# An attention block with an 8-bit product, written out without loops and with its fills cut into 16 parts a step

## The chip, the core and the metric

The kernel runs on one core of one Trainium2 chip. The time is device microseconds from start to end of one execution. Times given "at x" are microseconds from the start of the span of one profiled execution. Engines are named as in the profile: PE is TensorE (PEld its weight loads), DVE is VectorE, ACT is ScalarE, POOL is GpSimd, SP is SyncE, whose queue starts most DMAs.

## What is computed

For each of 8 batches `x` is 512 tokens by 256 features, and `cond` holds two style vectors `s1` and `s2`. Cut to what matters:

```python
x = x * s1[:, None, :]
x = (x - mu) * rsqrt(var + EPS_IN)                  # per token
q = heads(einsum('bsh,oh->bso', x, q_weight) * q_dc[:, None, :])
k = heads(einsum('bsh,oh->bso', x, k_weight) * k_dc[:, None, :])
v_flat = einsum('bsh,oh->bso', x, v_weight) * v_dc[:, None, :] * s2[:, None, :]
attn = softmax(einsum('bhqd,bhkd->bhqk', q, k) * scale)       # 16 heads of 16
out = einsum('bhqk,bhkd->bhqd', attn, heads(v_flat))...
out = einsum('bsh,oh->bso', out, w_weight) * w_dc[:, None, :]
y = out + einsum('bsh,oh->bso', v_flat, u_weight) * u_dc[:, None, :]
# y is rounded to int8 per token, rhs to int8 per column; their product is scaled back
return x_in + int8_product(y, rhs)
```

## The kernel before

The work is in 8 steps, one batch each, after a prologue. All five engines run programs of their own and meet at counting semaphores. Each engine works strictly in the order of its own program.

**A step** `t` has 16 rounds, 4 for each group of 4 heads. A round `r` has on PE `scores_of` (L939: four products into four PSUM banks, in two units of two), which I write S, and `values_of` (L953: four products that add to `o_acc`), which I write V. ACT takes the exponential of each unit of S (L493) into `probs`. The scores of a unit may be overwritten when its exponential is done, so S of round r+1 needs the exponentials of round r unit by unit. PE runs S of round r and then V of round r-1. `probs` has 2 buffers.

**Saving a group.** After the four rounds of a group ACT copies `o_acc` to `o_t` (`save_o`, L479), once V of the group's last round is done. It stands in ACT's program behind both exponentials of rounds 4, 8, 12 and of round 0 of the next step. V of the next group waits for it.

**Fills.** Behind V of certain rounds PE runs other work, the fills, through three banks of `work`. `claimed` lets PE be three uses ahead of DVE, which frees the banks in order. For the next batch, `a = t+1`: `xt` (the transposes of normalised x), `q` and `k` projections (L976, six products for one of two groups), `fold` (L985), `v` (L997, four token blocks of six products), `norms` (L1006) with a transpose of its maximum. For the batch before, `z = t-1`: `on` (16 transposes of `o_t` by token block, and DVE divides by the softmax sum), `ot` (back to features), `y` (L1087, the output projection), `yqt` (the transposed integers) and `ffn` (L1101, the integer product). All transposes are L815.

**Stacks.** ACT (L473) and DVE (L684, L688) split each q and k into a high and a low part in `parts`. SP copies these by 24 DMAs a batch (L322) into `q_stack` and `k_stack`, the operands of S. A flag, computed by DVE from the norms, says whether the scores are small enough to need no shift. If they are (they are here), SP copies zeros into two rows of `q_stack` (L311), between the third and fourth of its four lots of stack DMAs (the second and third in the prologue). The other branch, which computes row maxima, is jumped over.

**Loops.** Steps 1 to 6 are a loop of 3 turns with 2 steps in its body, on every engine; the prologue, step 0 and step 7 stand outside it. At the start of a step SP loads x of the next batch (L254), and DVE multiplies and measures it (L539, L545) before anything else of that step.

**The end.** Behind the last V, ACT saves the last group and the whole chain `on`, `ot`, `y`, `yqt`, `ffn`, residual (POOL, L439) and store of batch 7 runs with nothing beside it.

Of the kernel before, what the change touches and what calls it, by code (L numbers as in the profile page):

```python
# [5 lines left out]
F32 = mybir.dt.float32  # L20
# [7 lines left out]
P = 128  # L28
# [11 lines left out]
class Tally:  # L40

    def __init__(self, sem):
        self.sem, self.base, self.count = sem, 0, 0

    def value(self):
        return self.base + self.count

    def loop(self, index, per_turn):
        self.start, self.per_turn = self.value(), per_turn  # L50
        self.base, self.count = index * per_turn + self.start, 0

    def end_loop(self, turns):
        assert self.count == self.per_turn, (self.count, self.per_turn)
        self.base, self.count = self.start + turns * self.per_turn, 0

def adaln_ffn_kernel(nc, x, cond, wq, wk, wv, ww, wu, rhs, out):
# [15 lines left out]
    SETUP_USES, ROW_USES, RHS_USES, A_USES, Z_USES = 7, 2, 3, 12, 12  # L74
    STEP_USES = A_USES + Z_USES
# [3 lines left out]
    SHIFT = 2 * 2 * 16  # L79

# [4 lines left out]
    with ctx:  # L85
# [3 lines left out]
        def sem(name):  # L89
            return ctx.enter_context(nc.semaphore(name))  # L90

# [28 lines left out]
        col_now = sb("col_now", [P, 4])  # L120
# [11 lines left out]
        v_aug = sb("v_aug", [P, 2, KT, NH, DV])  # L132
# [6 lines left out]
        probs = sb("probs", [P, 2, 4, S])  # L139
        o_t = sb("o_t", [P, G, S])  # L140

# [8 lines left out]
        inv_den = sb("inv_den", [P, KT, NH])  # L150
        o_nat = sb("o_nat", [P, KT, H])
        o_t2 = sb("o_t2", [P, HC, S])
# [3 lines left out]
        y_scale = sb("y_scale", [P, KT])  # L156
        y_inv = sb("y_inv", [P, KT])
        y_q = o_nat
# [5 lines left out]

        by_two = [o_t2[:, :, :].rearrange("p c t -> p (c t)").rearrange("p (m c i) -> p m c i", m=2, c=HC),
# [16 lines left out]
        shift_loaded = sem("shift_loaded")  # L182
        pool_setup, const_ready = sem("pool_setup"), sem("const_ready")
# [5 lines left out]
        col_ready, wvs_ready, wd_ready = sem("col_ready"), sem("wvs_ready"), sem("wd_ready")  # L189
# [14 lines left out]

        FULL = ([("on", q) for q in range(KT)] + [("ot", i) for i in range(2)] + [("xt", c) for c in range(HC)]
                + [("rows", n) for n in range(ROW_USES)] + [("rhs", n) for n in range(RHS_USES)]
                + [("y", 0), ("y", 1), ("q", 0), ("k", 0), ("q", 1), ("fold", 0), ("k", 1), ("v", 0), ("bound", 0)]
                + [("v", k) for k in range(1, KT)] + [("yqt", i) for i in range(2)] + [("ffn", 0), ("ffn", 1)])
        A_KINDS = ("xt", "fold", "q", "k", "bound", "v")
        assert len(FULL) == STEP_USES + ROW_USES + RHS_USES  # L210

        def uses(has_a, has_z, prologue=False):
            def kept(kind):

                own = {"rows": prologue, "rhs": not prologue and not has_z}
                return own[kind] if kind in own else has_a if kind in A_KINDS else has_z

            return {u: n for n, u in enumerate([u for u in FULL if kept(u[0])])}

        def uses_before(t):  # L220

            return t * STEP_USES + (FIRST_STEP + A_USES + RHS_USES - STEP_USES)

        FIRST_STEP = SETUP_USES + A_USES + ROW_USES

        PAIRS = (B - 2) // 2

        def run_steps(eng, step, tally=None, per_turn=0):
            step(None, 0, has_a=True, has_z=False, base=SETUP_USES, bank=SETUP_USES, prologue=True)  # L230
            step(0, 0, has_a=True, has_z=False, base=FIRST_STEP, bank=FIRST_STEP)
            with eng.Fori(0, PAIRS) as pair:
                if tally is not None:
                    tally.loop(pair, per_turn)
                for odd in range(2):
                    t = pair * 2 + (1 + odd)
                    step(t, (1 + odd) % 2, has_a=True, has_z=True, base=uses_before(t), bank=uses_before(1 + odd))
            if tally is not None:
                tally.end_loop(PAIRS)
            step(B - 1, (B - 1) % 2, has_a=False, has_z=True, base=uses_before(B - 1), bank=uses_before(B - 1))  # L240

        LAST_Z = uses_before(B - 1) + Z_USES
        LAST_AT = {use: LAST_Z + n for n, use in enumerate(
            [("on", q) for q in range(KT)] + [("ot", 0), ("ot", 1), ("y", 0), ("y", 1), ("yqt", 0), ("ffn", 0),
                                              ("yqt", 1), ("ffn", 1)])}

        block = ctx.enter_context(nc.Block())

        @block.sync
        def _(sp):
# [7 lines left out]

            sp.sem_inc(res_added, 2)
# [5 lines left out]
            sp.wait_ge(demod_rows_ready, 1)  # L267
            sp.dma_start(rows_dram[:, :, :], demod_rows[:, :, :]).then_inc(rows_stored, 16)
            sp.wait_ge(rows_stored, 16)
            load_rows(0)  # L270
            sp.wait_ge(pool_stored, 16)
            sp.wait_ge(const_stored, 16)
            for par in range(2):
                for e in range(2):
                    sp.dma_start(k_stack[e * HALF + BIAS:e * HALF + ROWS, par, :, :].bitcast(F32), const_dram[1]
                                 ).then_inc(ones_loaded, 16)
            sp.wait_ge(xt_ready, 2)
            load_x(1)
# [6 lines left out]
            def step(t, par, has_a, has_z, base, bank, prologue=False):  # L285
                a = 0 if prologue else t + 1
                pa = 0 if prologue else 1 - par
                if has_a:
                    if not prologue:
                        wait(v_ready, a * KT)  # L290
                        wait(wd_ready, a)
                        if has_z:
                            wait(xt_ready, a * 2)
                            load_x(a)
                        load_rows(a)
                if has_z:
                    z = t - 1
                    wait(res_added, z * 2 + 2)
                    sp.dma_start(x_res[:, :, :], x[z].rearrange("(k p) h -> p k h", p=P)).then_inc(res_loaded, 16)
                if has_a:  # L300
                    if not prologue and not (isinstance(t, int) and t == 0):
                        wait(exp_done, t * UNITS)

                    for n in range(4):
                        if n == (2 if prologue else 3):

                            wait(flag_ready, a + 1)
                            small = sp.value_load(flag[0:1, 0:1], min_val=0, max_val=1)
                            with sp.If(small == 1):
                                for e in range(2):  # L310
                                    sp.dma_start(q_stack[e * HALF + BIAS:e * HALF + ROWS, pa, :, :].bitcast(F32),  # L311
                                                 const_dram[0]).then_inc(shift_loaded, SHIFT // 2)
                            sp.nop()
                        g, is_k = n // 2, n % 2
                        stack, which = (k_stack, K_PARTS) if is_k else (q_stack, Q_PARTS)
                        for part, part_ready in enumerate((hi_ready, low_ready)):
                            wait(part_ready, a * 4 + (n + 1))
                            for j in range(NB):
                                if which[j] == part:
                                    for e in range(2):  # L320
                                        rows_of = slice(e * HALF + j * D, e * HALF + (j + 1) * D)
                                        sp.dma_start(stack[rows_of, pa, g * GP:(g + 1) * GP, :].bitcast(F32),  # L322
                                                     parts[e * HALF:(e + 1) * HALF, n, part, :].bitcast(F32)
                                                     ).then_inc(stack_loaded[g], 16)
                    with sp.If(small == 0):
                        wait(shift_ready, a + 1)
                        for j in range(2):
                            for e in range(2):
                                row = e * HALF + BIAS + j
                                sp.dma_start(q_stack[row:row + 1, pa, :, :].bitcast(F32),  # L330
                                             shift[e * NP:(e + 1) * NP, j, :].bitcast(F32)
# [825 lines left out]
```

## Time and profile before

| what | value |
|---|---|
| median of 3 runs | 498.12 us (497.38 to 498.86) |
| the profiled execution's own time | 496.59 us |
| its span, first to last instruction | 494.9 us |
| mean granted TensorE clock | 0.962 |
| PE busy | 447.1 us (90%) |
| ACT busy | 290.1 us (59%) |
| DVE busy | 241.7 us (49%) |
| POOL busy | 103.6 us (21%) |

A group of instructions in a row has its start, its time from the first start to the last end, and in brackets how long its engine sat idle before it and what ended that wait.
### The profile page before, as it was taken

To read this page: it belongs to the slowest core of one execution; us is meant where nothing else is said; L and a number is where in the kernel's file an instruction comes from. 1 tells how busy PE (TensorE), PEld (TensorE's weight loads), DVE (VectorE), ACT (ScalarE), POOL (GpSimd) and SP (SyncE) were. 2 spreads that over 40 slices of the span, in tenths; PEclk is the share of its full clock that TensorE was granted. 3 is DMA by queue.
4 is the path that set the end of the run, shared out by engine and by line. 5 is a ranking of instruction groups with operands and counts; after the bars stand their busy time and mean duration, and the time that the engine had idled before them with its cause. 6 is when DMAs were issued, how large, how long until landed. Compare 5 with 4: busy or idle time off the path is not lost.

```text
span 494.9 us, 8739 instructions
## 1 busy us (share of the span) xinstructions
PE 447.1 (90%) x2626; PEld 225.3 (46%) x2626; DVE 241.7 (49%) x564; ACT 290.1 (59%) x333; POOL 103.6 (21%) x124
## 2 busy tenths in 40 slices
PE   6892899979999999969999999969999999999982
PEld 5771235434554455524454455424554455544251
DVE  4766142346444763446434763447444763444054
ACT  4030587556765766637765766647765766677930
POOL 5442003010121303031121303031121303020022
PEclk9997699998999999979999999989999999999997
DMA  6068309660497209650397209660497209620021
GB/s 208 0 149 176 68 1 137 109 146 1 62 129 159 88 20 134 107 177 0 57 130 145 105 12 139 107 182 0 64 128 158 87 22 135 106 88 1 1 86 42
DMA packets 29804, 45.31 MB, mean 92 GB/s; under 512 B 3928, under 2 KB 15448, under 8 KB 29704
## 3 DMA queue, kind: packets, MB, share of 16 engines
q1 hardware_dynamic: 27840, 40.02, 45.6%
q0 software_dynamic: 1072, 3.74, 1.9%
q8 instruction: 32, 0.52, 0.5%
q10 hardware_dynamic: 832, 0.80, 0.5%
q14 instruction: 28, 0.23, 0.2%
HBM read 15.09 MB, written 4.28 MB: 39 GB/s over the span
## 4 chain that ended last, share of the span: by engine, by line
PE 78%; issue 5%; ACT 5%; DMA 5%; DVE 5%; SPq 2%; POOL 1%; POOLq 0%; ACTq 0%; DVEq 0%
PE o_acc L953 22%; PE scores L939 16%; PE work L976 10%; PE work L997 9%; PE work L815 8%; PE work L1087 6%; ACT probs L493 4%; PE work L985 3%; DMA q_stack<-const_dram 2%; PE work L844 2%; PE work L1101 1%; DMA x_res<-in_L_cond_w_weight_dram 1%; DVE o_nat L749 1%; DMA rows<-in_cond_dram 1%; SPq L322 1%
## 5 line engine op out<-in xcount | busy, mean ns | idle before, releaser
L493 ACT ACTIVATE probs<-scores 128x1024 f32<-128x1024 f32 x256 | 247.9, 1026 | 129.0 <-PE scores L939 128.8
L953 PE MATMUL o_acc<-probs,v_aug 128*32 128x512 f32 x1024 | 140.7, 622 | 0.2
L939 PE MATMUL scores<-q_stack,k_stack 50*128 50x512 f32 x512 | 103.2, 467 | 26.7 <-DMA q_stack<-const_dram 10.9
L939 PEld LDWEIGHTS scores<-q_stack,k_stack 50*128 50x128 f32 x512 | 41.0, 191 | 81.9 <-issue 37.2
L420 POOL TENSOR_TENSOR squares<-parts 128x512 bf16<-128x512 f32 x32 | 33.3, 1041 | 185.5 <-ACT parts L473 185.5
L976 PE MATMUL work<-x_t,qk_w 128*128 128x512 f32 x192 | 54.3, 421 | 0.0
L997 PE MATMUL work<-vs_w,x_t 128*128 128x512 f32 x192 | 50.9, 407 | 0.3 <-DVEq L680 0.3
L439 POOL TENSOR_TENSOR res<-res,x_res 128x512 f32<-128x512 f32 x16 | 20.0, 1270 | 136.6 <-DVEq L799 136.6
L976 PEld LDWEIGHTS work<-x_t,qk_w 128*128 128x128 f32 x192 | 35.2, 193 | 24.1 <-issue 6.7
L997 PEld LDWEIGHTS work<-vs_w,x_t 128*128 128x128 f32 x192 | 34.2, 188 | 23.4 <-issue 13.9
L953 PEld LDWEIGHTS o_acc<-probs,v_aug 128*32 128x32 f32 x1024 | 20.5, 109 | 49.1 <-issue 45.5
L1087 PE MATMUL work<-w_demod,o_t 128*128 128x256 f32 x128 | 31.5, 390 | 0.0
L1087 PEld LDWEIGHTS work<-w_demod,o_t 128*128 128x128 f32 x128 | 23.1, 189 | 14.3 <-DVEq L767 5.0
L643 DVE TENSOR_TENSOR v_aug<-work,rows 128x256 f32<-128x256 f32 x32 | 13.5, 423 | 28.3 <-PE work L997 28.1
L688 DVE SCALAR_TENSOR_TENSOR parts<-work,col_now,parts 128x512 fp32r<-128x512 f32 x16 | 12.0, 751 | 30.7 <-ACT parts L473 27.2
L815 PE MATMUL work<-ident,o_t 128*128 128x128 f32 x136 | 21.1, 297 | 4.6 <-DVEq L752 2.8
L815 PEld LDWEIGHTS work<-ident,o_t 128*128 128x128 f32 x136 | 15.6, 149 | 19.6 <-issue 10.9
L815 PE MATMUL work<-ident,o_nat 128*128 128x128 f32 x128 | 19.6, 292 | 4.5 <-DVE o_nat L777 2.4
L473 ACT ACTIVATE parts<-work,col_now 128x512 fp32r<-128x512 f32 x16 | 11.0, 688 | 21.5 <-PE work L976 21.5
L782 DVE TENSOR_SCALAR y_qt<-work 128x512 bf16<-128x512 f32 x14 | 9.7, 691 | 28.3 <-PE work L815 26.1
L815 PEld LDWEIGHTS work<-ident,o_nat 128*128 128x128 f32 x128 | 14.3, 145 | 18.9 <-DVEq L752 7.1
L539 DVE TENSOR_TENSOR x_sb<-x_sb,rows 128x1024 f32<-128x1024 f32 x8 | 10.5, 1312 | 24.0 <-DMA rows<-in_cond_dram 12.6
(110 smaller groups left out, 389.4 us busy)
## 6 DMA issues: line engine op xcount, KB each, us to landing
q_stack<-parts SPq DMA_DIRECT2D x96, 128.0 KB, 5.3
k_stack<-parts SPq DMA_DIRECT2D x96, 128.0 KB, 5.5
x_sb<-in_x_dram SPq DMA_DIRECT2D x8, 512.0 KB, 5.4
x_res<-in_x_dram SPq DMA_DIRECT2D x8, 512.0 KB, 3.9
out_dram<-res POOLq DMA_DIRECT2D x7, 512.0 KB, 4.7
rows<-rows_dram SPq DMA_DIRECT2D x8, 384.0 KB, 5.5
rows<-in_cond_dram SPq DMA_DIRECT2D x8, 128.0 KB, 5.3
q_stack<-const_dram SPq DMA_DIRECT2D x16, 32.0 KB
```

Source lines behind the costliest of these rows:

```text
L420: nc.gpsimd.tensor_tensor(squares[:, n, :], parts[:, n, 0, :], parts[:, n, 0, :], ALU.mult).then_inc(squares_ready, 1)
L439: nc.gpsimd.tensor_tensor(res[:, two, :], res[:, two, :], x_res[:, two, :], ALU.add).then_inc(res_added, 1)
L493: nc.scalar.activation(probs[:, r % 2, pair:pair + 2, :], scores[:, pair:pair + 2, :], ACT.Exp).then_inc(exp_done, 1)
L643: nc.vector.tensor_tensor(v_aug[:, pa, k, :, 0:D], both[:, 0:H].rearrange("p (h d) -> p h d", d=D), rows[:, 1, :].rearrange("p (h d) -> p ...
L688: nc.vector.scalar_tensor_tensor(parts[:, n, 1, :], bank_qk, col_now[:, g:g + 1], parts[:, n, 0, :], ALU.mult, ALU.subtract).then_inc(low_ ...
L815: return nc.tensor.transpose(dst, src, ident[0:rows, 0:rows])
L939: last = nc.tensor.matmul(scores[:, 2 * (u % 2) + e, :], k_stack[top:top + ROWS, par, 2 * g + u % 2, kt * P:(kt + 1) * P], q_stack[top:top ...
L953: last = nc.tensor.matmul(o_acc[DV * j:DV * (j + 1), :], v_aug[:, par, kt, 4 * g + j, :], probs[:, r % 2, j, :], start=(kt == 0), stop=(kt ...
L976: last = nc.tensor.matmul(bank, lhs, right, start=(n == 0), stop=(n == len(operands) - 1))
L985: last = nc.tensor.matmul(bank[:, hc * H:(hc + 1) * H], wv_scaled[:, c, hc * P:(hc + 1) * P], w_t[WU][:, c, :], start=(c == 0), stop=(c == ...
L997: last = nc.tensor.matmul(bank, lhs, right, start=(n == 0), stop=(n == len(operands) - 1))
L1087: last = nc.tensor.matmul(bank[:, k * H:(k + 1) * H], lhs, right, start=(n == 0), stop=(n == len(operands) - 1))
```

## The change

- All loops are gone: each engine's program is written out for 8 steps. Waits are on constants.
- The 16 rounds are handled as 8 pairs `i`. In a pair PE runs S of round 2i, V, the first part of a fill, then `second_round()` (S of round 2i+1 and V), then the second part. So all 16 gaps between rounds can hold a part, listed in `fill`.
- V is one round later: behind S of round r comes V of round r-2. `probs` has 3 buffers.
- `save_o` in pairs 2, 4, 6 and in pair 0 stands between the exponentials of the two rounds of the pair.
- Of a batch's values only block 0 is projected in the step before; blocks 1 to 3 come in pairs 0 and 1 of its own step, just before V needs them. `v_aug` has one buffer instead of two.
- `on` goes by head group: four transposes as soon as a group is saved, so groups 0 to 2 are handled in their own step (pairs 3, 5, 7) and group 3 in pair 0 of the next. DVE's `normalise` takes a group for all tokens.
- `ffn` of a batch moves a step later (pairs 4 and 5 of step z+2).
- x of batch t+2 is loaded in step t, multiplied, measured and normalised there, so that `xt` in pair 1 finds it ready.
- SP writes the zeros at the start of a step whatever the flag says, and at the end of its stack DMAs only adds to the semaphore if the flag is set.

The core of the diff (of both programs only the lines that the text speaks of):

```diff
-        probs = sb("probs", [P, 2, 4, S])
+        probs = sb("probs", [P, RING, 4, S])
...
-        run_steps(pe, step)
...
-                for r in range(ROUNDS):
-                    scores_of(t, par, r, has_z)
-                    if r > 0:
-                        values_of(t, par, r - 1, has_z)
...
+            for t in range(B):
+                for i in range(SUPER):
+                    r = t * ROUNDS + 2 * i
+                    scores_of(r)
+                    if r > 0:
+                        values_of(r - 2)
+
+                    def second_round():
+                        scores_of(r + 1)
+                        if r > 0:
+                            values_of(r - 1)
+
+                    fill(t, i, second_round)
...
+                elif i == 2:
...
+                        if not first:
+                            to_features(z, 0)
+                        projected("q", a, 0)
+                        second_round()
+                        projected("k", a, 0)
...
+                elif i == 4:
...
+                        if y >= 0:
+                            int_product(y, 0)
+                        projected("k", a, 1)
+                        second_round()
+                        if not first:
+                            output(z, 0)
...
+                elif i == 6:
...
+                        if not first:
+                            quantised_transposed(z, 0)
+                            output(z, 1)
+                        second_round()
+                        norms(a)
...
-                    if r % KT == 0 and r > 0:
-                        save_o(t, r // KT - 1)
-                    if r == 0 and has_z:
-                        save_o(t - 1, G - 1)
...
+                for i in range(SUPER):
+                    exponentials(t * ROUNDS + 2 * i)
+                    if i == 0 and t > 0:
+                        save_o(t * G - 1)
+                    if i in (2, 4, 6):
+                        save_o(t * G + i // 2 - 1)
+                    exponentials(t * ROUNDS + 2 * i + 1)
```

Three places show how the instructions move. **ACT, rounds 0 to 9 of step 0** (`probs` is written by the exponentials, two for a round; `o_t` by `save_o`; `parts` are the high parts), before:

```order
L493 ACTIVATE probs<-scores 128x1024 x10
L479 ACTIVATE o_t<-o_acc 128x512
L493 ACTIVATE probs<-scores 128x1024 x6
L473 ACTIVATE parts<-work,col_now 128x512
L493 ACTIVATE probs<-scores 128x1024 x2
L479 ACTIVATE o_t<-o_acc 128x512
L473 ACTIVATE parts<-work 128x512
L493 ACTIVATE probs<-scores 128x1024 x2
```

and now:

```order
L473 ACTIVATE probs<-scores 128x1024 x10
L481 ACTIVATE o_t<-o_acc 128x512
L473 ACTIVATE probs<-scores 128x1024 x2
L463 ACTIVATE parts<-work,cols 128x512
L463 ACTIVATE parts<-work 128x512
L473 ACTIVATE probs<-scores 128x1024 x4
L463 ACTIVATE parts<-work,cols 128x512
L473 ACTIVATE probs<-scores 128x1024 x2
L481 ACTIVATE o_t<-o_acc 128x512
L473 ACTIVATE probs<-scores 128x1024 x2
```

The save of group 0 stands behind the ten exponentials of rounds 0 to 4 in both. But V of round 3, for which it waits, stood on PE behind S of round 4, and stands now behind S of round 5, whose exponentials come behind the save. Both high parts of q and k group 0 now follow round 5.

**PE, the same step at the rounds from 0 on** (S is `scores<-`, V is `o_acc<-`), before:

```order
L939 MATMUL scores<-q_stack,k_stack 128x512 x8
L953 MATMUL o_acc<-probs,v_aug 32x512 x4
L939 MATMUL scores<-q_stack,k_stack 128x512 x4
L953 MATMUL o_acc<-probs,v_aug 32x512 x4
L815 MATMUL work<-ident,x_sb 128x128 x8
```

and now:

```order
L887 MATMUL scores<-q_stack,k_stack 128x512 x4
L944 MATMUL work<-vs_w,x_t 128x512 x6
L887 MATMUL scores<-q_stack,k_stack 128x512 x4
L944 MATMUL work<-vs_w,x_t 128x512 x6
L887 MATMUL scores<-q_stack,k_stack 128x512 x4
L901 MATMUL o_acc<-probs,v_aug 32x512 x4
L944 MATMUL work<-vs_w,x_t 128x512 x6
L887 MATMUL scores<-q_stack,k_stack 128x512 x4
L901 MATMUL o_acc<-probs,v_aug 32x512 x4
L864 MATMUL work<-ident,x_sb 128x128 x8
```

Value blocks 1, 2 and 3 of the running batch now stand in the step itself, and the first V behind the third S.

**SP, the prologue** (stack DMAs in lots of six, the flag's load, the zeros from `const_dram`), before:

```order
L258 DMA rows<-rows_dram 128x768
L275 DMA k_stack<-const_dram 2x4096 x4
L254 DMA x_sb<-in_x_dram 128x4x256
L255 DMA rows<-in_cond_dram 128x256
L322 DMA q_stack<-parts 16x4x512 x6
L322 DMA k_stack<-parts 16x4x512 x6
L308 TENSOR_LOAD flag
L308 ISA x2
L309 COMPARE_AND_BRANCH
L311 DMA q_stack<-const_dram 2x4096 x2
L309 UNCONDITIONAL_BRANCH
L322 DMA q_stack<-parts 16x4x512 x6
```

and now:

```order
L248 DMA q_stack<-const_dram 2x4096 x2
L290 DMA k_stack<-const_dram 2x4096 x4
L293 DMA rows_dram<-o_nat 8x768
L231 DMA x_sb<-in_x_dram 128x4x256
L232 DMA rows<-in_cond_dram 128x256
L235 DMA rows<-rows_dram 128x768
L261 DMA q_stack<-parts 16x4x512 x6
L261 DMA k_stack<-parts 16x4x512 x6
L261 DMA q_stack<-parts 16x4x512 x6
L261 DMA k_stack<-parts 16x4x512 x6
L268 TENSOR_LOAD flag
```

The zeros went ahead of everything, and the flag is read only behind all 24 stack DMAs.

## Rows read from the trace of the kernel before

**Rows 1.** The page's fourth part: shares of the chain that ended last.

```profile
PE 78%; issue 5%; ACT 5%; DMA 5%; DVE 5%; SPq 2%; POOL 1%; POOLq 0%; ACTq 0%; DVEq 0%
```

**Rows 2.** Windows: step 0; steps 1 to 6; step 6; step 7; the tail.

```profile
core 0: us, PE busy (x) PEld busy (x) DVE busy (x) ACT busy (x) POOL busy (x), PEclk, DMA share, GB/s
51.08:99.40 48.32, 46.47 (x265) 20.55 (x266) 15.75 (x34) 33.94 (x39) 5.56 (x6) 0.93 0.51 77
99.40:432.92 333.52, 317.98 (x1907) 154.59 (x1903) 171.22 (x399) 211.22 (x241) 68.25 (x75) 0.97 0.54 96
...
380.44:432.92 52.48, 51.84 (x319) 25.33 (x318) 28.84 (x68) 35.05 (x40) 11.94 (x13) 1.00 0.54 99
432.92:473.80 40.88, 38.89 (x257) 15.16 (x256) 13.44 (x33) 32.14 (x36) 3.42 (x4) 1.00 0.08 27
473.80:494.90 21.10, 10.09 (x60) 7.05 (x56) 10.56 (x28) 2.98 (x5) 5.71 (x5) 0.83 0.21 75
```

**Rows 3.** Timeline of PE, first rounds of step 6.

```profile
380.44 0.73 PE L939 MATMUL scores<-q_stack,k_stack 50*128 50x512 f32 x4
381.10 1.06 PE L953 MATMUL o_acc<-probs,v_aug 128*32 128x512 f32 x8
382.14 0.50 PE L939 MATMUL scores<-q_stack,k_stack 50*128 50x512 f32 x2
383.05 0.49 PE L939 MATMUL scores<-q_stack,k_stack 50*128 50x512 f32 x2 [0.41 <-ACT probs L493]
383.59 1.06 PE L953 MATMUL o_acc<-probs,v_aug 128*32 128x512 f32 x8
```

**Rows 4.** Timeline of PE in steps 1 and 2: fills.

```profile
117.35 1.09 PE L815 MATMUL work<-ident,x_sb 128*128 128x128 f32 x8
...
176.92 1.99 PE L1087 MATMUL work<-w_demod,o_t 128*128 128x256 f32 x8
178.85 0.73 PE L939 MATMUL scores<-q_stack,k_stack 50*128 50x512 f32 x4
...
180.51 1.67 PE L976 MATMUL work<-x_t,qk_w 128*128 128x512 f32 x6
182.10 0.73 PE L939 MATMUL scores<-q_stack,k_stack 50*128 50x512 f32 x4
```

**Rows 5.** Timeline of PE: a loop's turn, and step 1's late x.

```profile
214.95 1.22 PE L939 MATMUL scores<-q_stack,k_stack 50*128 50x512 f32 x4 [4.51 <-issue]
...
109.69 1.11 PE L815 MATMUL work<-ident,o_t 128*128 128x128 f32 x4 [2.80 <-DVEq L752]
```

**Rows 6.** Timeline, the last V and its save; ACT in step 2.

```profile
472.79 1.06 PE L953 MATMUL o_acc<-probs,v_aug 128*32 128x512 f32 x8
473.93 0.60 ACT L479 ACTIVATE o_t<-o_acc 128x512 f32<-128x512 f32 x1 [1.29 <-PE o_acc L953]
...
160.37 0.60 ACT L479 ACTIVATE o_t<-o_acc 128x512 f32<-128x512 f32 x1
160.84 1.96 ACT L493 ACTIVATE probs<-scores 128x1024 f32<-128x1024 f32 x2
```

**Rows 7.** Timeline of DVE in step 1: the split of both `xt` banks.

```profile
118.05 0.69 DVE L532 CAST x_t<-work 128x512 fp32r<-128x512 f32 x1 [1.45 <-PE work L815]
120.51 0.69 DVE L533 TENSOR_TENSOR x_t<-work,x_t 128x512 fp32r<-128x512 f32 x1
```

**Rows 8.** Timeline of SP in the prologue; then one piece of the chain, in order of time.

```profile
30.51 3.90 SPq L322 DMA_DIRECT2D q_stack<-parts  x6
34.52 3.77 SPq L322 DMA_DIRECT2D k_stack<-parts  x6
...
45.11 3.99 SPq L322 DMA_DIRECT2D k_stack<-parts  x6
...
39.84 11.19 DMA q_stack<-const_dram
```

**Rows 9.** Timeline of PE in the tail: the output projection.

```profile
479.48 2.76 PE L1087 MATMUL work<-w_demod,o_t 128*128 128x256 f32 x12
```

More of the change, by code:

```diff
@@ L40, with __init__, step_fills @@
 class Tally:
[L43 to L55, printed above, removed]
+    def __init__(self):
+        self.count = 0
+def step_fills(t, last):
+    a, z, y = t + 1, t - 1, t - 2
+    if t == 0:
+        return [[("v", t, 1), ("v", t, 2)],
+                [("v", t, 3), ("xt", a, 0), ("xt", a, 1)],
+                [("q", a, 0), ("k", a, 0)],
+                [("on", t, 0), ("rhs", 0, 0), ("q", a, 1)],
+                [("k", a, 1)],
+                [("on", t, 1), ("fold", a, 0), ("rhs", 0, 1)],
+                [("norms", a, 0)],
+                [("v", a, 0), ("on", t, 2), ("rhs", 0, 2)]]
+    if t == last:
+        return [[("v", t, 1), ("v", t, 2), ("on", z, 3)],
+                [("v", t, 3), ("ot", z, 0), ("ot", z, 1)],
+                [("ffn", y, 0), ("y", z, 0)],
+                [("ffn", y, 1), ("on", t, 0), ("y", z, 1)],
+                [("yqt", z, 0)],
+                [("on", t, 1), ("yqt", z, 1)],
+                [("ffn", z, 0)],
+                [("on", t, 2), ("ffn", z, 1)]]
+    ffn = [[("ffn", y, n)] if y >= 0 else [] for n in range(2)]
+    return [[("v", t, 1), ("v", t, 2), ("on", z, 3)],
+            [("v", t, 3), ("xt", a, 0), ("xt", a, 1)],
+            [("ot", z, 0), ("q", a, 0), ("k", a, 0)],
+            [("ot", z, 1), ("on", t, 0), ("q", a, 1)],
+            ffn[0] + [("k", a, 1), ("y", z, 0)],
+            ffn[1] + [("on", t, 1), ("fold", a, 0)],
+            [("yqt", z, 0), ("y", z, 1), ("norms", a, 0)],
+            [("v", a, 0), ("on", t, 2), ("yqt", z, 1)]]
 def adaln_ffn_kernel(nc, x, cond, wq, wk, wv, ww, wu, rhs, out):
@@ L79, in adaln_ffn_kernel @@
     SHIFT = 2 * 2 * 16
+    ORDER = ([("cond", 0, 0)] + [("weight", 0, m) for m in range(5)] + [("sums", 0, 0)]
+             + [("xt", 0, 0), ("xt", 0, 1), ("rows", 0, 0), ("rows", 0, 1)]
+             + [("q", 0, 0), ("k", 0, 0), ("q", 0, 1), ("fold", 0, 0), ("k", 0, 1), ("norms", 0, 0), ("v", 0, 0)])
+    PROLOGUE_USES = len(ORDER)
+    USES_BY = []
+    for t in range(B):
+        for fill in step_fills(t, B - 1):
+            ORDER += fill
+        USES_BY.append(len(ORDER))
+    ORDER += ([("on", B - 1, 3), ("ot", B - 1, 0), ("ot", B - 1, 1), ("y", B - 1, 0), ("y", B - 1, 1)]
+              + [("yqt", B - 1, 0), ("yqt", B - 1, 1), ("ffn", B - 1, 0), ("ffn", B - 1, 1)])
+    USE = {key: n for n, key in enumerate(ORDER)}
+    assert len(USE) == len(ORDER)
     const_dram = nc.dram_tensor("const_dram", (2, 2, NP, S), F32).ap()
@@ L202, in adaln_ffn_kernel @@
         spare = sem("spare")
[L205 to L246, printed above, removed]
         block = ctx.enter_context(nc.Block())
@@ L276, in _ @@
                                  ).then_inc(ones_loaded, 16)
+            sp.wait_ge(demod_rows_ready, 1)
+            sp.dma_start(rows_dram[:, :, :], demod_rows[:, :, :]).then_inc(rows_stored, 16)
             sp.wait_ge(xt_ready, 2)
             load_x(1)
-            def wait(semaphore, value):
-                sp.wait_ge(semaphore, value)
-                sp.sem_inc(spare, 1)
[L285 to L301, printed above, removed]
-                        wait(exp_done, t * UNITS)
[L304 to L331, printed above, removed]
-                                             ).then_inc(shift_loaded, 16)
-                    sp.nop()
@@ L514, in _ @@
         @block.vector
         def _(dve):
-            chain = Tally(dve_step)
+            chain, taken = Tally(), Tally()
             def link(instruction):
@@ L812, in _ @@
+            product(B - 1, 1)
         @block.tensor
@@ L1015, in values_and_maxima @@
[L1015 to L1024 removed]
+                bank = claim("xt", a, c)
@@ new lines, in norms, with norms_transposed @@
+            def norms(a):
+                pe.wait_ge(squares_ready, a * 4 + 4)
+                bank = claim("norms", a, 0)
+                for n in range(4):
+                    last = nc.tensor.matmul(bank[32 * n:32 * (n + 1), :], head_ones[:, :], squares[:, n, :],
+                                            start=True, stop=True)
+                last.then_inc(norms_summed, 1)
+            def norms_transposed(a):
+                pe.wait_ge(norms_ready, a + 1)
+                bank = work[:, USE[("norms", a, 0)] % NW, :]
+                transpose(bank[0:1, 0:P], norm_max[:, :]).then_inc(work_ready, 1)
@@ new lines, in _ @@
+            last.then_inc(work_ready, 1)
+            x_transposed(0, 0)
+            x_transposed(0, 1)
+            pe.wait_ge(demod_ready, 1)
+            for n, ms in enumerate(((WV, WW), (WU,))):
+                bank = claim("rows", 0, n)
+                for i, m in enumerate(ms):
+                    for g in range(HC):
+                        last = transpose(bank[0:B, i * H + g * P:i * H + (g + 1) * P], demod[:, m * HC + g, :])
+                last.then_inc(work_ready, 1)
+            for _ in range(4):
+                nc.tensor.matmul(scores[:, 0, 0:P], ones[:, :], ident[:, :], start=True, stop=True)
@@ new lines, in _ @@
+            projected("q", 0, 0)
+            projected("k", 0, 0)
+            projected("q", 0, 1)
+            skip_matrix(0)
+            projected("k", 0, 1)
+            norms(0)
+            norms_transposed(0)
+            values(0, 0)
+            row_maxima(0, PROLOGUE_USES)
+            for t in range(B):
+                for i in range(SUPER):
[8 more added lines that the diff above has]
+                    fill(t, i, second_round)
```

1158 lines of the change are left out of this document (631 added, 527 removed).

## The prediction

> **What bounds the kernel now.** I read the chain that ended last first: 78% of it is PE [rows 1]. The windows by step then say how full PE is. Step 6, with nothing odd in it, takes 52.48 us at full clock with PE busy 51.84 [rows 2]; steps 1 to 6 together take 333.5, which is 18.6 more than six times step 6. ACT has 35 us of work in step 6 and DVE 29, so neither is the limit on average. The question for the change is therefore only where PE stands still, before and after.
>
> Counting pitches: S costs 0.66 and V 1.0 [rows 3], a q, k or value block 1.59 (180.51 to 182.10), an output projection 1.93 (176.92 to 178.85), eight transposes 1.02, so four 0.51 [rows 4]. Sixteen rounds are 16 x 1.66 = 26.5. The fills are `on` 2.0, `ot` and `xt` 1.0 each, `y` 3.9, q and k 6.4, `fold` 1.8, values 6.2, norms 0.5, and for `yqt` and `ffn` 1.0 each (the last five by likeness to the rows): 24.8. The sum is 51.3, so step 6 stands still for about 1.2 to 1.3. Two thirds of that are in round 1, which has no fill ahead of it: V is at 383.59 where 382.10 + 0.66 was possible, 0.83 lost to exponentials [rows 3].
>
> **What it removes.** Each term is a difference to the profiled execution.
>
> 1. The two turns of the loop: PE stands still 4.51 before 214.95, and S then takes 1.22 where 0.73 is usual, a clock of 1.2 GHz in place of 2.4 [rows 3, 5]. Step 1 waits 2.80 for DVE, behind an x that came late, and is slow afterwards as well [rows 5]. Together these are the 18.6 above [rows 2]. Straight-line code has no turn, and x is loaded a step earlier: **-18.6**. That straight code costs nothing of its own I take from step 6: it is the second in the loop's body, has 1.3 for all its waits, and so no such gap within it [rows 2].
> 2. Rounds without a fill: 1.2 in each of steps 1 to 6, about 2.4 in step 0 and 4.5 in step 7 (40.88 against 17 V, 16 S and 8.9 of fills; [rows 2]): **-14**.
> 3. The prologue. S of step 0 starts at 51.03, when the zeros issued at 39.84 have landed [rows 8]. They now go first. What remains is SP's issuing: a lot of six DMAs took 4.0 (30.51 to 34.52), the later ones 4.0 to 4.9. The second lot behind the flag ended at 49.10. Without the zeros and the wait for the flag between the lots, and starting some 2 us earlier, 24 DMAs end near 45, and the flag's load adds 1. S starts near 46: **-5.1**. From both sides: -7 if the DMAs are issued without the slow lot, 0 if the landing of the parts is what really takes until 51.
> 4. The tail: four saved groups used to be transposed and divided behind the last V, now one. The output projection started 5.7 behind the last V's end (479.48, [rows 9]) and starts at about 3.5 now. The rest of the 21.1 [rows 2] stays: **-2.1**.
>
> **What it moves.** Value blocks 1 to 3 of batch 0 ran in the prologue, hidden behind the DMA wait, and now run in step 0: 3 x 1.55 = 4.6. The three groups of `on` of batch 7 that left the tail are 1.5 in step 7: **+6.2**. PE has the same matmuls otherwise.
>
> **What it adds: the save in front of an exponential.** V of a group's last round stood right behind S of the next; now it stands behind S of the round after that, and ACT's program has the save ahead of that round's exponentials. Let that S start at T. V starts at T+0.66. The save started 1.14 after the start of V, and the next exponential 0.47 after the save (160.37 to 160.84) [rows 6]: save at 1.80, exponential at 2.27. One takes 1.02 and two 1.96, so they end at 3.29 and 4.23. The first unit of the next S can start at 3.3, the second at 4.3, and V came 0.54 behind a second unit that had waited (383.05 to 383.59, [rows 3]): 4.8. With nothing in the way V would start at T + 1.66 + f + 0.66, f being the second part of the fill. So each save costs 2.5 - f.
>
> - Pair 0: f is a value block and four transposes, 2.1: 0.4.
> - Pair 2: f is k, 1.59: 0.9.
> - Pair 4: f is the output projection, 1.93: 0.6.
> - Pair 6: f is the norms, 0.3: 2.2.
>
> That is 4.1 in each of steps 1 to 6. Step 0 has no pair 0 save and nothing in pair 4: 5.6. Step 7 has nothing in pairs 4 and 6: 6.0. Sum: 24.6 + 5.6 + 6.0 = **+36**. Before, the cover was the order itself: V followed at once, and the save ran beside a fill. From both sides: 0 if ACT somehow had V's result earlier, which nothing in the order allows, and 45 if f counts for nothing in pairs 0 and 4.
>
> **Smaller waits.** DVE's splits of `xt` ended 3.85 behind the start of those transposes (117.35 to 121.20, [rows 4, 7]). Between `xt` and q now stand S, V and four transposes: 1.02 + 2.17 = 3.2, so q waits 0.7, in step 0 1.2: **+5.8**. In pair 3 both high parts (about 0.55 each) stand ahead of the next exponentials: 0.25 a step, with thin first parts in steps 0, 1 and 7 some 1.2 more: **+3**. Elsewhere DVE has the time: its 29 us a step [rows 2] are spread over a step of 55. One place is tight. In pairs 6 and 7 it measures x, rounds one half, quantises the other and reduces the norms, some 7 us in a row, before PE can go on to value block 0. Alone that would hold PE for about 1 a step (an allowance, not a row); behind the save's 2.2 it costs nothing.
>
> The jump over the row maxima, one in each step, stays as it is; it must lie within the 1.3 us of all waits of step 6 [rows 2]. The Trainium skill's "Runtime: NRT & Kernel Launch", section "Instruction fetch mechanics", says that a taken branch whose target is outside the pages at hand stalls for a fetch. For the loop's turn the trace agrees with its 4.51. If the jumps were such branches too, removing the two turns would be the smaller part of what branches cost, and eight times 4.5 would stay; the sum goes by the row.
>
> **Sum.** -18.6 - 14 - 5.1 - 2.1 + 6.2 + 36 + 5.8 + 3 = +11.2. The profiled execution took 496.59 and becomes 507.8; its span of 494.9 becomes 506. The median of the runs, 498.12, is 1.5 above it, so I say **509** (2.2% slower).
>
> **Rivals.**
>
> - *The save does not reach PE* (faster). If PE is held elsewhere so long, in the fill behind each save, that the exponentials are there anyway, the 36 fall away, the allowance of 1 a step in pair 7 appears (8), and the time is 498.1 + 11.2 - 36 + 8 = 481. Half of the 36 gives 491. It decides from 25 of the 36 down. Against it: both engines run strictly in order, and PE, not ACT, is full. Chance with all versions of it 0.2.
> - *The clock falls in the stalls.* In pair 6 PE is idle from T + 1.66 + 0.3 to 3.3 and most of the time to 4.3. A wait of 2.80 had halved the clock, one of 0.41 not [rows 3, 5]. Of the 18.6, two turns at 4.5 and the 2.80 leave 6.8 for three slow stretches, 2.3 each. If the clock falls in each of 8 steps: +18, 527. Chance 0.08. The Trainium skill's "TensorE: Matmul & The Clock Gate", section "A second HAM failure mode: psum-queue depth-cycling", tells of a kernel whose short idle times between groups of matmuls made the clock swing; that speaks for this case, the rounds with 0.41 speak against it.
> - *Late stacks.* SP now reads the flag behind all stack DMAs, and issues zeros, x and rows ahead of them. If their landing or issuing is late for S of the next step, each step start waits some 2: +14, 523. Against: k of group 1 is projected in pair 4, half a step early. Chance 0.08.
> - *No difference*: the terms of both signs are large and may cancel, with the save at 25 instead of 36. Chance 0.06.
>
> The forecast itself has 0.58. Its own bounds: the prologue 0 to -7, the save 29 to 42, the rest +-3, so 500 to 517. The range over all cases is **491 to 525**. A measurement of this kernel can tell about 0.3% from no change. Faster 0.2, same 0.06, slower 0.74.
>
> **What will show it.** Right: no wait of PE named issue above 1 us; S of step 0 at 46; steps 1 to 6 at 55 to 57 each; four saves a step that waited for V, with the exponential behind them starting 2.3 after its S, and PE waiting for ACT in pair 6 for 2 us in two pieces; the tail at 19. Wrong: steps at 52 or less with ACT's saves not waiting, a granted clock under 0.93, or waits of DVE that I have not listed. The least sure numbers are the prologue's DMA landing and f in pair 6.

## The result and the profile after

The changed kernel takes 516.3 us (median of 4 runs, 509.72 to 520.89), the kernel before 498.49. Two of the four, 518.27 and 520.89, lie more than 1.5% above the quickest and are left out of every comparison below; the other two, 509.72 and 514.32, have the median 512.0. That is 1.027 times before, with a 95% interval of 1.019 to 1.036. So the change makes the kernel slower; by how much, two runs tell only roughly. The forecast was 509, in a range of 491 to 525, and both medians lie in it. The profiled execution took 514.32 us, with a span of 512.4.

The four runs of the changed kernel lie 11 us apart, those of before beside them 2. But eleven further runs of before went from 493.70 to 502.79. What spreads the runs is not shown: the quickest, 509.72, had a granted clock of 0.954, no higher than the 0.958 of the profiled one.

The shares of the chain that ended last, from the profile's page:

```profile
PE 70%; ACT 13%; DVE 6%; issue 4%; SPq 3%; DMA 2%; ACTq 0%; POOL 0%; POOLq 0%; DVEq 0%
```

And what ended PE's longest waits (us in total, times, longest):

```profile
PE scores L887 <- ACT probs L473: 23.6, 35, 1.6
PE scores L887 <- SPq L270: 7.3, 1, 7.3
PE work L923 <- DVEq L567: 5.1, 7, 1.2
```

ACT's share of the chain went from 5% [rows 1] to 13%. No wait of PE is named issue any more, so the loop's turns are gone. In their place PE waits 35 times for exponentials.

Windows: step 0, steps 1 to 6, steps 2 and 3, step 7, the tail:

```profile
45.76:102.81 57.05, 51.11 (x270) 23.53 (x270) 23.26 (x53) 34.30 (x39) 11.39 (x13) 0.88 0.53 81
102.81:441.61 338.80, 319.56 (x1897) 154.65 (x1896) 167.08 (x389) 208.78 (x240) 64.66 (x66) 0.98 0.56 91
157.94:215.26 57.32, 54.11 (x319) 26.44 (x318) 28.76 (x68) 34.80 (x40) 11.88 (x12) 0.97 0.56 94
215.26:271.06 55.80, 52.60 (x319) 25.49 (x318) 28.76 (x68) 34.79 (x40) 11.82 (x12) 1.00 0.57 96
441.61:492.44 50.83, 46.46 (x291) 19.62 (x290) 17.68 (x42) 32.67 (x36) 5.29 (x5) 0.97 0.07 26
492.44:512.40 19.96, 8.96 (x45) 6.39 (x44) 7.85 (x20) 2.88 (x5) 3.81 (x4) 0.77 0.22 80
```

Against [rows 2]: the start gained 5.3 us (45.76 against 51.08), step 0 is 8.7 longer, steps 1 to 6 are 5.3 longer together (338.8 against 333.5) although both turns of the loop are gone, step 7 is 10.0 longer, the tail 1.1 shorter. Only part of step 7's 10.0 is waiting: value blocks 1 to 3 of the last batch, one more V, and `ffn` of batch 5, all run in it now and ran in earlier steps before. A step without a slow stretch takes 55.80, where step 6 of before took 52.48.

This is pair 6 of steps 2 and 3, by PE's timeline, and ACT in the first of them:

```profile
204.41 1.07 PE L901 MATMUL o_acc<-probs,v_aug 128*32 128x512 f32 x8
205.29 0.40 PE L952 MATMUL work<-squares,head_ones 128*32 128x512 bf16 x4
207.11 0.50 PE L887 MATMUL scores<-q_stack,k_stack 50*128 50x512 f32 x2 [1.42 <-ACT probs L473]
208.03 0.50 PE L887 MATMUL scores<-q_stack,k_stack 50*128 50x512 f32 x2 [0.42 <-ACT probs L473]
208.46 1.07 PE L901 MATMUL o_acc<-probs,v_aug 128*32 128x512 f32 x8
209.45 0.34 PE L864 MATMUL work<-ident,norm_max 128*1 128x128 f32 x1
209.48 2.87 PE L944 MATMUL work<-vs_w,x_t 128*128 128x512 f32 x6
...
265.79 1.07 PE L901 MATMUL o_acc<-probs,v_aug 128*32 128x512 f32 x8
266.78 0.27 PE L864 MATMUL work<-ident,norm_max 128*1 128x128 f32 x1
266.81 1.65 PE L944 MATMUL work<-vs_w,x_t 128*128 128x512 f32 x6
...
205.54 0.60 ACT L481 ACTIVATE o_t<-o_acc 128x512 f32<-128x512 f32 x1 [3.28 <-PE o_acc L901]
206.04 3.77 ACT L473 ACTIVATE probs<-scores 128x1024 f32<-128x1024 f32 x4
```

The predicted sequence is there piece by piece. S of the pair's second round began at 203.75, 0.66 before V. V starts at 204.41, the save 1.13 later, the exponential 0.50 behind the save, and the next S can start only at 207.11 and 208.03. V is at 208.46, T + 4.71, where the forecast had 4.8. ACT itself had stood idle for 3.28 us in front of the save.

What I had given a small chance is the next line: the value block at 209.48 takes 2.87, and the same one a step later 1.65. Behind the wait the clock had fallen in step 2 and not in step 3.

Steps 4 and 6 have such a slow stretch as well, and steps 1 and 5 have none. There are three more outside the steps 1 to 6: in step 0 behind the saves of pairs 4 and 6, and in step 7 behind that of pair 6. From steps 0 and 7, where an S at full clock takes 0.73:

```profile
83.65 1.22 PE L887 MATMUL scores<-q_stack,k_stack 50*128 50x512 f32 x4
97.14 2.91 PE L944 MATMUL work<-vs_w,x_t 128*128 128x512 f32 x6
487.45 1.22 PE L887 MATMUL scores<-q_stack,k_stack 50*128 50x512 f32 x4
```

By the lengths of the steps a slow stretch costs 1.5 to 1.6 us in steps 2, 4 and 6 (57.32, 57.35 and 57.40 against 55.80). By the pitches of their products the first of step 0 costs some 3, the second and that of step 7 some 1.5 each. Together that is an estimate of some 10 us in this execution.

### The profile page after: what moved, and what is told of

The parts are those of the page before. It is cut to its first block, busy times and chain, and to the rows that moved or that the text cites. A ratio compares the mean times of both kernels' runs of the same rounds, so it can differ in the third digit from the quotient of the medians.

```text
span 512.4 us, 7640 instructions
## 1 busy us (share of the span) xinstructions
PE 455.9 (89%) x2626; PEld 229.2 (45%) x2626; DVE 242.9 (47%) x564; ACT 288.5 (56%) x333; POOL 100.5 (20%) x116
## 4 chain that ended last, share of the span: by engine, by line
PE 70%; ACT 13%; DVE 6%; issue 4%; SPq 3%; DMA 2%; ACTq 0%; POOL 0%; POOLq 0%; DVEq 0%
PE o_acc L901 24%; PE scores L887 15%; ACT probs L473 12%; PE work L944 8%; PE work L864 7%; PE work L923 6%; SPq L261 3%; PE work L1015 3%; PE work L932 3%; DVE x_t L536 2%; DVE x_t L535 2%; PE work L1029 2%; PE work L1174 2%; DMA x_res<-in_L_cond_w_weight_dram 1%; DMA rows_dram<-o_nat 0%
## 5 line engine op out<-in xcount | busy, mean ns | idle before, releaser
L481 ACT ACTIVATE o_t<-o_acc 128x512 f32<-128x512 f32 x32 | 19.1, 597 | 92.2 <-PE o_acc L901 92.2
L944 PE MATMUL work<-vs_w,x_t 128*128 128x512 f32 x192 | 59.8, 453 | 0.0
L944 PEld LDWEIGHTS work<-vs_w,x_t 128*128 128x128 f32 x192 | 38.1, 213 | 26.4 <-DVEq L655 5.9
L923 PEld LDWEIGHTS work<-x_t,qk_w 128*128 128x128 f32 x192 | 34.1, 190 | 26.9 <-issue 7.5
L580 DVE SCALAR_TENSOR_TENSOR parts<-work,cols,parts 128x512 fp32r<-128x512 f32 x16 | 12.0, 750 | 58.9 <-ACT parts L463 58.9
L864 PE MATMUL work<-ident,o_t 128*128 128x128 f32 x200 | 32.7, 294 | 5.6 <-DVE o_t L675 3.7
L864 PEld LDWEIGHTS work<-ident,o_t 128*128 128x128 f32 x200 | 23.7, 148 | 26.4 <-issue 17.8
L575 DVE TENSOR_TENSOR parts<-work,parts 128x512 fp32r<-128x512 f32 x16 | 11.1, 692 | 34.5 <-ACT parts L463 32.9
L650 DVE RECIPROCAL inv_den<-work 128x16 f32<-128x16 f32 x32 | 8.2, 258 | 30.7 <-PE work L864 26.6
L463 ACT ACTIVATE parts<-work,cols 128x512 fp32r<-128x512 f32 x16 | 11.1, 694 | 16.0 <-PE work L923 16.0
L691 DVE SCALAR_TENSOR_TENSOR res<-work,y_scale,rhs_scale_row 128x256 f32<-128x256 f32 x32 | 14.0, 479 | 8.7 <-PE work L1029 8.3
## 6 DMA issues: line engine op xcount, KB each, us to landing
x_sb<-in_x_dram SPq DMA_DIRECT2D x8, 512.0 KB, 3.7
x_res<-in_x_dram SPq DMA_DIRECT2D x8, 512.0 KB, 4.4
out_dram<-res POOLq DMA_DIRECT2D x7, 512.0 KB, 8.5
```

What stands on the lines that cost most here:

```text
L481: nc.scalar.activation(o_t[:, group % G, :], o_acc[:, :], ACT.Copy).then_inc(o_saved, 1)
L864: return nc.tensor.transpose(dst, src, ident[0:rows, 0:rows])
L923: last = nc.tensor.matmul(bank, lhs, right, start=(n == 0), stop=(n == len(operands) - 1))
L944: last = nc.tensor.matmul(bank, lhs, right, start=(n == 0), stop=(n == len(operands) - 1))
```

## Experiments

All times are medians of 6 runs with an interval against the kernel before on the same chip.

### The save behind both exponentials

```diff
                     exponentials(t * ROUNDS + 2 * i)
+                    exponentials(t * ROUNDS + 2 * i + 1)
                     if i == 0 and t > 0:
                         save_o(t * G - 1)
                     if i in (2, 4, 6):
                         save_o(t * G + i // 2 - 1)
-                    exponentials(t * ROUNDS + 2 * i + 1)
```

> The changed kernel with the save of a group behind both exponentials of a pair instead of between them; nothing else moves. Theory 1 (the save in front of an exponential is the cost): the waits of S for ACT in pairs 0, 2, 4 and 6, 24 us in total, go, and with them the stretches at 1.2 GHz behind pair 6; about 1 us a step comes back as a wait for DVE in pair 7 (norms transposed). Time 478 to 486. Rival (ACT is not the cause, V one round late is, or the split of the fills is): the time stays over 505.

479.7 us, 0.964 times before (0.959 to 0.968). PE's waits in this run:

```profile
PE work L864 <- DVE norm_max L607: 4.3, 6, 0.8
...
PE scores L887 <- ACT probs L473: 2.6, 11, 0.4
```

and the same pair 6 as above:

```profile
193.98 0.40 PE L952 MATMUL work<-squares,head_ones 128*32 128x512 bf16 x4
194.31 0.50 PE L887 MATMUL scores<-q_stack,k_stack 50*128 50x512 f32 x2
194.97 0.50 PE L887 MATMUL scores<-q_stack,k_stack 50*128 50x512 f32 x2 [0.16 <-ACT probs L473]
195.46 1.07 PE L901 MATMUL o_acc<-probs,v_aug 128*32 128x512 f32 x8
197.23 0.27 PE L864 MATMUL work<-ident,norm_max 128*1 128x128 f32 x1 [0.71 <-DVE norm_max L607]
```

S now follows the norms at once, and no step has a slow stretch behind pair 6. Moving one ACT instruction past two others, 31 times in the program, is worth 512.0 - 479.7 = 32.3 us by the medians and 512.4 - 478.3 = 34.1 by the spans of the two profiles. It turns a kernel 2.7% slower than before into one 3.6% faster. Of the six waits for the reduced norms one, of 0.8, is in the prologue and stood in the changed kernel too. The other five, 3.5 in total, are in pair 7 of steps 1 to 5, as the forecast had allowed for.

Step 3 of both runs, compared V by V, tells what each save costs. In the changed kernel the V behind pair 0's save comes 7.95 us after the step's start, here 7.61; behind pair 2's 22.50 and 21.35, behind pair 4's 36.28 and 34.47, behind pair 6's 50.53 and 47.02. Taken apart, with 0.2 for pair 3, the four saves cost 0.3, 0.8, 0.5 and 1.7, or 3.3 a step, where the forecast had 0.4, 0.9, 0.6 and 2.2, or 4.1.

### V one round earlier, the save left where it was

```diff
-                        values_of(r - 2)
+                        values_of(r - 1)
...
                         scores_of(r + 1)
-                        if r > 0:
-                            values_of(r - 1)
+                        values_of(r)
...
-            values_of(B * ROUNDS - 2)
             values_of(B * ROUNDS - 1)
```

> The changed kernel with V of round r-1 behind S of round r, as before the change; the save stays between the two exponentials of a pair. Theory 1: V of a group's last round is then done when ACT comes to the save, so this takes the same 24 us of waits away as moving the save: 478 to 488. Rival (the position of the save in ACT's program is costly by itself): over 505.

479.1 us, 0.963 (0.958 to 0.968), the same as the experiment above; PE's S waits for ACT 2.4 us in all. So neither the place of the save nor the lag of V costs anything alone that these runs can tell. It is the two together: a save that stands in front of an exponential while the V that it needs stands behind the S of that exponential.

### The kernel before without its loop

```diff
-            with eng.Fori(0, PAIRS) as pair:
...
+            for t in range(1, B - 1):
+                step(t, t % 2, has_a=True, has_z=True, base=uses_before(t), bank=uses_before(t))
```

> The kernel before with its loop of three turns written out, nothing else. My term: two turns at 4.5 and two slow stretches behind them, 2.3 and 0.9 by the steps' lengths, so -12: 486 to 487. Step 1 keeps its late x. Rival (straight-line code fetches no faster, or stalls elsewhere): 495 to 500.

483.7 us, 0.972 (0.967 to 0.977): 14.6 under the kernel before beside it (498.28), 2.6 more than I expected. In the two profiles step 1 falls from 58.52 to 53.60, although its x is loaded no earlier in the program. Its wait for DVE was 2.80 with a slow clock behind it [rows 5], and is 1.45 here with none:

```profile
109.21 0.66 PE L809 MATMUL work<-ident,o_t 128*128 128x128 f32 x4
111.32 0.66 PE L809 MATMUL work<-ident,o_t 128*128 128x128 f32 x4 [1.45 <-DVEq L746]
```

What holds DVE is the same in both, the landing of `rows`. Its multiplication of x, with the loop and without:

```profile
105.41 1.23 DVE L539 TENSOR_TENSOR x_sb<-x_sb,rows 128x1024 f32<-128x1024 f32 x1 [9.10 <-DMA rows<-in_cond_dram]
107.10 1.22 DVE L533 TENSOR_TENSOR x_sb<-x_sb,rows 128x1024 f32<-128x1024 f32 x1 [7.72 <-DMA rows<-in_cond_dram]
```

That is 6.01 us after the start of step 1 with the loop and 4.63 without. SP started that load 0.55 behind the step's start with the loop (99.95) and 0.49 ahead of it without (101.98), so most of the 1.4 is SP being earlier.

Measured so, taking out the loop is worth 15 of the 18.5 us that separate the first experiment from the kernel before. All of the rest of the change together (fills in 16 parts, values late, `on` by group, x early, the zeros first) brings 4. Next to none of it is in the steady step: steps 2 to 6 take 52.3 to 52.6 here, and 52.3 with the save moved and the norms' wait gone (below).

### The second output projection behind pair 6's second round

```diff
                             quantised_transposed(z, 0)
-                            output(z, 1)
                         second_round()
+                        if not first:
+                            output(z, 1)
                         norms(a)
```

> The changed kernel with the second output projection behind the second round of pair 6 (steps 1 to 6), so that f there is 2.2 instead of 0.3. Theory 1 by itself: the wait for ACT in pair 6 (1.42 and 0.42) falls under 0.4, and 11 us would be gained. But DVE quantises this half before it reduces the norms, and now gets it later: I expect a wait of 1.5 to 2 us for the reduced norms in pair 7 in its place. With it 512 to 517, without it 500 to 506.

521.5 us, 1.045 (1.040 to 1.050): worse than the changed kernel (512.0) and outside my 512 to 517. PE's waits, and pairs 6 and 7 of step 3:

```profile
PE work L864 <- DVE norm_max L607: 13.3, 7, 2.2
PE scores L887 <- ACT probs L473: 12.1, 22, 1.6
```

```profile
261.78 1.99 PE L1015 MATMUL work<-w_demod,o_t 128*128 128x256 f32 x8
263.71 0.40 PE L952 MATMUL work<-squares,head_ones 128*32 128x512 bf16 x4
264.04 0.86 PE L887 MATMUL scores<-q_stack,k_stack 50*128 50x512 f32 x4
264.82 1.07 PE L901 MATMUL o_acc<-probs,v_aug 128*32 128x512 f32 x8
268.07 0.27 PE L864 MATMUL work<-ident,norm_max 128*1 128x128 f32 x1 [2.18 <-DVE norm_max L607]
268.17 2.21 PE L944 MATMUL work<-vs_w,x_t 128*128 128x512 f32 x6
270.31 1.22 PE L887 MATMUL scores<-q_stack,k_stack 50*128 50x512 f32 x4
```

The direction was right: with the longer second part the wait for ACT in pair 6 is gone, and the wait for DVE that I expected took its place. Its size was not: 2.18 in one piece, and behind it the clock fell (S at 270.31 takes 1.22). The same slow S stands behind the wait in steps 2, 3, 4 and 5 of this profile. It is not there in step 1, with the same wait, nor in step 6, where the wait is 1.6. Steps 1 to 6 take 343.5 together, 4.7 more than in the changed kernel. Another 3.9 of the 8.0 us between the two spans lie in step 7 and the tail, where the edit changes nothing: the clock fell behind both long waits of step 7 here. Half of a fill moved to cover one wait made the next one, and in sum nothing was gained.

### Products to fill the wait in pair 6

Products whose result is overwritten by the norms, so that PE is busy while it waits; they compute nothing that is used. First eleven, then six:

```diff
                 bank = claim("norms", a, 0)
+                if a > 1:
+                    for _ in range(6):
+                        nc.tensor.matmul(bank[:, 0:P], ones[:, :], ident[:, :], start=True, stop=True)
```

> The changed kernel with eleven added products of 128 x 128 ahead of the norms in pair 6 of steps 1 to 6, whose result is overwritten: PE has 1.4 us of work where it waited 1.42 for the exponential. If the slow stretches behind pair 6 (2.87 and 2.84 for a value block that takes 1.66) come from that idle time, they go and the steps of 57.3 become 55.8: 4 to 8 us less than the changed kernel, 507 to 511. If they come from something else, or the added work is not hidden, 515 to 525.

Eleven: 514.1 us, 1.032 (1.026 to 1.039), above my 507 to 511 and not apart from the changed kernel. They took 2.72 us, not 1.4. But the starts of steps 2 to 7 are 56.4 apart, every one: no stretch there is slow. So I repeated it with less work:

> As the run with eleven added products, with six: these took 0.24 us each and not 0.13, so eleven were 2.7 us, of which 1.4 were hidden, and every step took 56.4 where the changed kernel alternates between 55.8 and 57.4. Six are 1.4 us and fit the stall. If the idle time is what lets the clock fall: all steps 55.2 to 56.0, 507 to 511. If the removal of the slow stretches needed the longer work: steps of 57 and more stay, 514 and up.

Six: 509.4 us, 1.020 (1.014 to 1.026), in my 507 to 511. The added work (each of these products stands as two in the profile) and what follows it in step 2:

```profile
205.03 1.60 PE L953 MATMUL work<-ident,ones 128*128 128x128 f32 x12
206.57 0.40 PE L955 MATMUL work<-squares,head_ones 128*32 128x512 bf16 x4
206.90 0.50 PE L887 MATMUL scores<-q_stack,k_stack 50*128 50x512 f32 x2
207.65 0.50 PE L887 MATMUL scores<-q_stack,k_stack 50*128 50x512 f32 x2 [0.25 <-ACT probs L473]
208.08 1.06 PE L901 MATMUL o_acc<-probs,v_aug 128*32 128x512 f32 x8
209.08 0.27 PE L864 MATMUL work<-ident,norm_max 128*1 128x128 f32 x1
209.10 1.64 PE L944 MATMUL work<-vs_w,x_t 128*128 128x512 f32 x6
```

The value block takes 1.64, and the starts of steps 2 to 7 in this run (157.52, 213.35, 269.16, 324.95, 380.73, 436.51) are 55.8 apart, each of them. In the changed kernel they alternate between 57.3 to 57.4 and 55.8. Steps 0 and 7, where nothing was added, keep their slow stretches in this profile (S at 84.05 and at 482.19 takes 1.22). The slow stretches of steps 2, 4 and 6 therefore come from the idle time in pair 6. Filling it gains the 4.7 us that they cost in the profile of the changed kernel. The medians, 512.0 and 509.4, don't settle it by themselves: the runs here go from 506.67 to 512.31, and one of the changed kernel's took 509.72.

### Measuring x later, and reading the flag earlier

Two steps on top of the first experiment. DVE's `measure()` moves behind value block 0 of pair 7:

```diff
-                if a + 1 < B:
-                    measure()
                 if z >= 0:
                     integers(z, 0)
...
                 v_and_skip(a, 0)
+                if a + 1 < B:
+                    measure()
                 normalise(t, 2)
```

> The changed kernel with the save behind both exponentials, and DVE measuring the next x behind value block 0 of pair 7 instead of ahead of the quantising in pair 6. The run with the save alone moved had six waits of PE for the reduced norms, 0.7 to 0.8 each, 4.3 in total: my allowance of 1 a step. They should go: 474 to 477. If normalising that x becomes late instead, xt waits in pair 1 and the time stays near 480.

476.0 us, 0.953 (0.948 to 0.957), in my 474 to 477; of the waits for the reduced norms only the 0.8 of the prologue is left. Then, in the prologue only, the flag is read between the second and third lot of stack DMAs:

```diff
                 for n in range(4):
+                    if a == 0 and n == 2:
+                        wait(flag_ready, 1)
+                        small = sp.value_load(flag[0:1, 0:1], min_val=0, max_val=1)
+                        with sp.If(small == 1):
+                            sp.sem_inc(shift_loaded, SHIFT)
...
                 with sp.If(small == 1):
-                    sp.sem_inc(shift_loaded, SHIFT)
+                    if a > 0:
+                        sp.sem_inc(shift_loaded, SHIFT)
...
```

> The run before, and in the prologue SP reads the flag between the second and third lot of stack DMAs. PE waited 7.4 us for SP's count behind the fourth lot. If only the order on SP holds it, S of step 0 starts at 40 to 42 instead of 45.8 and the time falls by 3 to 5, to 470 to 473. If the landing of the first two lots holds it (my bound of 0 for that term), it falls by under 1.

471.9 us, 0.945 (0.941 to 0.950), the fastest kernel here. S of step 0:

```profile
42.32 0.99 PE L896 MATMUL scores<-q_stack,k_stack 50*128 50x512 f32 x4 [3.46 <-DMA k_stack<-parts]
```

It starts at 42.32, where the run before had 46.48, and is now held by the landing of the second lot, for 3.46 us. So SP's order was the limit in the changed kernel. My bound of 0 for the prologue's term, in which the landing takes until 51, is refuted: the parts had landed by 42.3.

## Why the prediction held, and where its sizes were off

The forecast held, but in part by luck: the largest term was too large, and an effect that the sum had at nothing made up for it.

- **The save, +36.** The step that decided, and right in its mechanism: T + 4.71 in pair 6 against 4.8. Its size was lower, 3.3 in each of steps 1 to 6 in place of 4.1. With steps 0 and 7, read from the same profiles without their slow stretches, I estimate 28 for all of it, just under my own bounds of 29 to 42. Most of the error is pair 6, 1.7 and not 2.2: without the save S and V do not follow there as closely as I had assumed. That moving the save gained 32 to 34 us does not confirm the 36, because that figure has the clock in it, less the 3.5 of waits for the norms that came back.
- **The clock, 0 in the sum.** The rival of the falling clock I had given 0.08 and +18. It came true in part, together with the main case and not instead of it: six slow stretches in the profiled execution, in five of the eight steps, some 10 us. The error was to treat it as all or nothing, and as excluded by the rounds with 0.41. The stated range did not even hold this rival's own 527.
- **The loop and the late x, -18.6.** The loop alone measured -14.6 (expected -12). In its profile steps 1 to 6 take 315.7 against 333.5, so nearly the whole 18.6 went with the loop, while x kept its place in the program. The earlier load of x is not shown to have gained anything of its own.
- **Rounds without fills, -14, and smaller waits, +8.8.** For a step the two nearly cancel, -1.2 against 0.7 and 0.25, and the steady step bears it out: 52.48 before, 52.30 with the save and the norms out of the way. In step 0 the gain did not show: 49.29 in that run against 48.32 before. The waits of q for `xt` are 5.1 in the profile after, against 5.8; its parts add up to 5.4 (six times 0.7, and 1.2). My allowance of 1 us a step for the norms, hidden behind the save, came out as 0.7 a step once the save was moved, and removing it gained 3.8 in all.
- **What moved, +6.2.** The sum is right, its place is not. Step 0 has four value blocks in both kernels; the three more are in step 7, which before had none.
- **The prologue, -5.1.** Measured -5.3, by the mechanism named: SP's count behind the fourth lot.
- **The tail, -2.1.** Measured -1.1. The output projection starts 3.6 behind the last V, as forecast, but what follows takes 16.4 and not 15.4.
- **The page on a swinging clock.** "TensorE: Matmul & The Clock Gate" of the Trainium skill, section "A second HAM failure mode: psum-queue depth-cycling", tells of a kernel in which short idle times between groups of matmuls made the clock swing between its two levels. The trace agrees in kind, with 1.42 and 0.42 us of idle time in each pair 6 of steps 0 to 6 and a value block at 2.87 instead of 1.65 behind some of them. That these idle times come from the banks in which products are collected, as there, no run here shows; they are waits for ACT.
- **The rival of the hidden save** has fallen: PE had nothing else to wait for in those places. **Late stacks** did not occur in any step after the first.

Not settled: why the same wait lets the clock fall in some steps and not in others, and what spreads the runs of the changed kernel.

## What to carry to other kernels

When one engine's product is moved a stage later, go through every program that waits for it and look at what is queued behind that wait. Here a copy stood in front of an exponential that the next product needed, and 31 such places cost 6% of the time. A stall of PE has to be priced with the clock behind it. And filling one stall by moving work from ahead of it makes whoever consumed that work late: follow its consumer first.

## What the runs showed of the hardware

- Idle pieces of 1.42 and 0.42 us, with 0.5 of work between, stand in pair 6 of steps 0 to 6 of the changed kernel. Behind them PE's clock fell to 1.2 GHz in steps 0, 2, 4 and 6 and not in 1, 3 and 5, for a loss of some 1.5 us each. Behind pieces of 1.63 and 0.4 it fell in two of three places.
- The same place filled with 1.6 us of work: never, in any of the six steps where it was filled.
- A single piece of 2.18 (the second output projection moved) let it fall in four of five steps. One of 1.6 in the same run did not, and one of 1.45 (the kernel before without its loop, step 1) did not either.
- At the two turns of a loop whose body is two steps long, on all five engines, PE stood still 4.51 [rows 5] and 4.77 us; without the loop the kernel took 14.6 us less. The second turn:

```profile
327.08 0.96 PE L939 MATMUL scores<-q_stack,k_stack 50*128 50x512 f32 x4 [4.77 <-issue]
```
